# Expert tiles of a mixture-of-experts layer loaded and stored in pairs, their slots interleaved in DRAM

## The reference, cut to what matters

```python
xn = layernorm(x)                                   # 2048 tokens x 256
router = sigmoid(xn @ gate_w)                       # 16 experts
selected = top_k(router + expert_bias, 2)           # two experts for each token
top_scores = router[selected] / sum                 # their weights
shared = silu(xn @ sg_w) * (xn @ su_w) @ sd_w       # one expert that every token takes
for e in range(16):
    g, u = split(xn @ experts_gate_up[e])           # 256 -> 2 x 128
    routed += comb[:, e] * (silu(g) * u @ experts_down[e])
return x + attention(xn) + shared + routed
```

## Time and profile before

| | |
|---|---|
| time, median of 3 runs | 526.53 us (524.24 to 529.89) |
| profiled execution, time and span | 525.04 us, 523.2 us |
| PE busy | 461.9 us (88%) |
| DVE busy | 324.3 us (62%) |
| ACT busy | 249.4 us (48%) |
| POOL busy | 198.4 us (38%) |
| `x_in<-sorted_tokens` | 48 loads of 128 KB, median 2.7 us from issue to landing |
| `sorted_outputs<-y_out` | 48 stores of 128 KB, median 1.7 us |

### The profile page before, as it was taken

One profiled execution on the slowest core, in us unless ns is written; L12 is line 12 of the kernel. 1 busy time (PEld: TensorE's weight loads), 2 busy tenths in 40 slices (PEclk: granted clock), 3 DMA queues, 4 the chain that ended last, 5 costly groups with the idle time before them and its releaser, 6 DMA issues.

```text
span 523.2 us, 9031 instructions
## 1 busy us (share of the span) xinstructions
PE 461.9 (88%) x3049; PEld 271.6 (52%) x3050; DVE 324.3 (62%) x610; ACT 249.4 (48%) x567; POOL 198.4 (38%) x239
## 2 busy tenths in 40 slices
PE   4595999737859999995999999999999999999998
PEld 4454788525635666763445354444444444332676
DVE  3869985413425656676867877778586867744232
ACT  2620652112213333332767676676676757678300
POOL 3470777699940000006888888800000000000000
PEclk9799799977779999997999999999999999999999
DMA  9898999799999434424113333221120000010022
GB/s 282 188 403 256 318 323 291 246 170 144 188 174 203 127 110 121 130 79 140 42 49 104 108 86 106 71 76 61 48 82 18 3 3 3 1 13 6 3 89 73
DMA packets 65705, 64.60 MB, mean 123 GB/s; under 512 B 21935, under 2 KB 59539, under 8 KB 65635
## 3 DMA queue, kind: packets, MB, share of 16 engines
q1 hardware_dynamic: 51506, 47.85, 30.9%
q0 software_dynamic: 13056, 15.83, 15.0%
q10 hardware_dynamic: 1104, 0.41, 0.3%
HBM read 37.27 MB, written 27.13 MB: 123 GB/s over the span
## 4 chain that ended last, share of the span: by engine, by line
PE 66%; DVE 13%; DMA 12%; issue 2%; ACT 2%; POOL 2%; SPq 1%; POOLq 0%; DVEq 0%
PE ps L1248 12%; PE ps L1222 10%; PE ps L1234 10%; PE ps L1147 7%; PE ps L1268 5%; DMA x_in<-sorted_tokens 5%; DVE mx L970 5%; PE ps L1043 4%; PE ps L1163 4%; DMA ks<-aux_rows 2%; PE ps L1237 2%; PE ps L1223 2%; PE ps L1137 2%; ACT pt L718 2%; DMA x_sb<-x 1%
## 5 line engine op out<-in xcount | busy, mean ns | idle before, releaser
L718 ACT ACTIVATE pt<-ps 128x512 f32<-128x512 f32 (+3 forms) x384 | 167.1, 494 | 79.7 <-PE ps L1237 55.2
L970 DVE TENSOR_REDUCE mx<-ps 128x1 f32<-128x384 f32 (+6 forms) x189 | 153.3, 863 | 52.4 <-PE ps L1223 51.1
L1248 PE MATMUL ps<-pt,vg 128*32 128x512 f32 (+3 forms) x768 | 71.9, 492 | 0.0
L575 POOL DMA_INDIRECT yg<-sorted_outputs,slot_i x32 | 32.0, 1000 | 94.2 <-DMA sorted_outputs<-y_out 85.4
L1147 PE MATMUL ps<-w_gu,hx 128*128 x192 | 58.3, 432 | 3.8 <-issue 2.2
L1234 PE MATMUL ps<-qs,ks 111*128 111x512 bf16 (+3 forms) x192 | 55.7, 331 | 3.7 <-DMA qs<-nr 3.0
L1234 PE MATMUL ps<-qk 111*128 111x512 bf16 (+3 forms) x192 | 54.9, 329 | 1.8 <-ACT pt L718 0.3
L935 DVE COPY y_out<-ps 128x256 f32<-128x256 f32 x48 | 20.4, 425 | 56.4 <-PE ps L1163 52.7
L1237 PE MATMUL ps<-cbf 128*128 128x128 bf16 x256 | 52.4, 221 | 0.0
L691 ACT ACTIVATE hx<-ps 128x384 f32<-128x384 f32 (+1 forms) x48 | 22.9, 477 | 61.3 <-PE ps L1137 58.6
L1222 PE MATMUL ps<-qk 108*128 108x512 bf16 (+3 forms) x192 | 50.2, 328 | 1.8 <-DVE mx L970 1.3
(11 more groups left out here) (175 smaller groups left out, 737.9 us busy)
## 6 DMA issues: line engine op xcount, KB each, us to landing
sorted_tokens<-y_out SPq DMA_DIRECT2D x12, 512.0 KB, 5.0
qk_parts<-parts SPq DMA_DIRECT2D x16, 384.0 KB, 3.5
x_in<-sorted_tokens SPq DMA_DIRECT2D x48, 128.0 KB, 2.7
sorted_outputs<-y_out SPq DMA_DIRECT2D x48, 128.0 KB, 1.7
w_gu<-e_gu SPq DMA_DIRECT2D x1, 2816.0 KB, 12.9
x_sb<-x SPq DMA_DIRECT2D x4, 512.0 KB, 8.4
w_dn<-e_dn SPq DMA_DIRECT2D x1, 2048.0 KB, 8.7
y<-x_sb SPq DMA_DIRECT2D x16, 128.0 KB, 1.7
```

The source lines that it names most:

```text
L575: g_.indirect_dma_start(out=yg[:, n % 4, :], out_offset=None, in_=ysd, in_offset=bass.IndirectOffsetOnAxis(ap=slot_i[:, k, t:t + 1], axis= ...
L718: sc.activation(pt[:, s % 4, j, lo:CH], bank(n % 3)[:, lo:CH], ACT.Exp).then_inc(s_exp, 1)
L970: last = v.reduce_max(dst, src, axis=AX.X)
L1248: ins = te.matmul(ps[32 * j:32 * j + 32, OUT_BANK * CH + lo:(OUT_BANK + 1) * CH], vg[:, par, kb, j, :], pt[:, s % 4, j, lo:CH], start=kb = ...
```

## The change: two tiles to a transfer

Two consecutive tiles (2m and 2m + 1) share a block of 256 rows in DRAM. Before, slot s is row s. Now row 2p + b of the block belongs to partition p of tile 2m + b, so that one partition's two rows lie side by side, 2 KB. VectorE computes the new row number from the slot with integer operations (5 more instructions than the cast before), SP loads and stores two tiles with one DMA each, and there are two semaphores for the loads and two for the stores where there were four of each. The buffers stay four; a pair of them is loaded, and stored, at once. The gather reads the same rows through `slot_i`.

```diff
+            slot_n = tmp("slot_n", [P, 3, K_TOP, TT], I32)
...
-        s_xin = [sem(f"tile_loaded{i}") for i in range(4)]
+        s_xin = [sem(f"tile_pair_loaded{i}") for i in range(2)]
...
-        s_ys = [sem(f"tile_out_stored{i}") for i in range(4)]
+        s_ys = [sem(f"tile_pair_stored{i}") for i in range(2)]
...
-            def load_tile(k, u):
-                sp.dma_start(x_in[:, u, :], xsd[bass.ds(k * P, P), :]).then_inc(s_xin[u], DMA)
-
-            def store_tile(k, u):
-                sp.wait_ge(s_yo, k + 1)
-                sp.dma_start(ysd[bass.ds(k * P, P), :], y_out[:, u, :]).then_inc(s_ys[u], DMA)
-
-            for k in range(4):
-                load_tile(k, k)
+            def load_tiles(k, half):
+                sp.dma_start(x_in[:, 2 * half:2 * half + 2, :],
+                             xsd[bass.ds(k * P, 2 * P), :].rearrange("(p k) d -> p k d", k=2)).then_inc(s_xin[half], DMA)
+
+            def store_tiles(k, half):
+                sp.wait_ge(s_yo, k + 2)
+                sp.dma_start(ysd[bass.ds(k * P, 2 * P), :].rearrange("(p k) d -> p k d", k=2),
+                             y_out[:, 2 * half:2 * half + 2, :]).then_inc(s_ys[half], DMA)
+
+            for half in range(2):
+                load_tiles(2 * half, half)
...
-            def next_tile(k, u):
-                sp.wait_ge(s_hxt, k - 3)
-                load_tile(k, u)
-
-            for k in range(4, 7):
-                next_tile(k, k % 4)
+            def next_tiles(k, half):
+                sp.wait_ge(s_hxt, k - 2)
+                load_tiles(k, half)
+
+            next_tiles(4, 0)
             with sp.Fori(0, NT // 4 - 2) as i:
-                for u in range(4):
-                    next_tile(i * 4 + u + 7, (u + 3) % 4)
-                    store_tile(i * 4 + u, u)
-            next_tile(NT - 1, 3)
-            for k in range(NT - 8, NT):
-                store_tile(k, k % 4)
+                for half in range(2):
+                    next_tiles(i * 4 + 2 * half + 6, 1 - half)
+                    store_tiles(i * 4 + 2 * half, half)
+            next_tiles(NT - 2, 1)
+            for k in range(NT - 8, NT, 2):
+                store_tiles(k, k // 2 % 2)
...
-                v.tensor_copy(slot_i[:, :, :], slot_f[:, :, :]).then_inc(s_slot, 1)
+                then(v.tensor_copy(slot_n[:, 0, :, :], slot_f[:, :, :]))
+                then(v.tensor_scalar(slot_n[:, 1, :, :], slot_n[:, 0, :, :], P - 1, 1,
+                                     ALU.bitwise_and, ALU.logical_shift_left))
+                then(v.tensor_scalar(slot_n[:, 2, :, :], slot_n[:, 0, :, :], 7, 1,
+                                     ALU.logical_shift_right, ALU.bitwise_and))
+                then(v.tensor_tensor(slot_n[:, 1, :, :], slot_n[:, 1, :, :], slot_n[:, 2, :, :], ALU.bitwise_or))
+                then(v.tensor_scalar(slot_n[:, 0, :, :], slot_n[:, 0, :, :], 8, 8,
+                                     ALU.logical_shift_right, ALU.logical_shift_left))
+                v.tensor_tensor(slot_i[:, :, :], slot_n[:, 0, :, :], slot_n[:, 1, :, :], ALU.bitwise_or
+                                ).then_inc(s_slot, 1)
...
-                    dve.wait_ge(s_ys[u], stored)
+                    dve.wait_ge(s_ys[u // 2], stored)
...
-                pe.wait_ge(s_xin[u], need)
+                pe.wait_ge(s_xin[u // 2], need)
```

More of the change, by code:

```diff
@@ L563, in _ @@
                         load(pool, side, g, half)
-            for u in range(4):
-                pool.wait_ge(s_ys[u], NT // 4 * DMA)
+            for stored in s_ys:
+                pool.wait_ge(stored, NT // 4 * DMA)
             pool.wait_ge(s_sha, TT // 2)
```

## The result

Over four runs of each on the same chip the changed kernel takes 538.17 us (534.75 to 540.67), the kernel before 525.38 us (523.81 to 529.89): ratio 1.0225, 95% interval 1.0132 to 1.0318. The forecast was 525.5 us with a range of 515 to 533; the time lies outside it, on the side of rival B and beyond its price. The profiled execution took 540.67 us, the longest of the four, with a span of 538.8 against 523.2; so the two profiles lie 15.6 us apart where the medians lie 12.8 apart.

The account below looks back on a forecast made before the run. Mostly PE bound it, with tile loads waiting beside POOL's queue early in the tile stage. 525.04 + 1.05 (slots) - 1.2 (paired loads) = 524.9, or 526.4 on the median's scale; stated 525.5 us, range 515 to 533.

Parts of the forecast that it names:

- rival B: SP's ring of two pairs: lost look-ahead outweighs the gain, landing takes 12.7 us; slower, 533 us, chance 0.20.
- What bounds the kernel: Chain mostly PE, 66%; tile loads matter only at the tile stage's start, beside POOL's queue, 5% of the span.
- four tiles take L' + 2.3 (a step) + 0.4: Crowded tile stage: paired landing time plus one step plus SP and transpose, 12.4 us per four tiles; gain 1.2 us.
- L': A paired load's time to landing in the crowded part, taken as 9.7 us, between 7.2 and 12.7.
- Tile 8 itself: First paired load in the crowd: issued at about 122.0, landing 10.4 us later, tile 8 at 132.4.
- The step: Time from a pair's first tile to its second on PE, taken as 2.3 us.
- Rival A: DMA queues taking turns by packet: pairs drain faster, landing falls to 7.2 us; faster, 517 us, chance 0.33.
- Rival C: SP's queue cuts each 2 KB into 1 KB packets, landing stays 14.4 us; slower, 534 us, chance 0.05.
- The slots, +1.05 us: Five added VectorE instructions before the scatter, 0.21 us each, delay the path in full by 1.05 us.
- First scores until 118: PE's first attention scores would wait for POOL's loads until 118 us, neither much longer nor shorter.
- The quiet part, 0: From tile 20 on PE sets the pace; paired loads and stores land within three steps, so no effect, 0.
- Stores: Under rival B: DVE may wait for a paired store issued one step later; no size of its own.

Follow-up runs that it names:

- e9: The kernel before with six input buffers in place of four, single tiles loaded six steps ahead: 522.66 us, ratio 0.9956 to the kernel before.
- e4: The kernel before, layout and 1 KB packets kept, with two single-tile loads issued together as a pair, stores likewise: 532.47 us, ratio 1.0132.
- e2: The changed kernel with loads in pairs but stores of single tiles: 537.03 us, ratio 1.0182 to the kernel before.
- e10: The kernel before with six input buffers and POOL's loads spread over the stage: 511.89 us, ratio 0.9761 to the kernel before.
- e3: The changed kernel with stores in pairs but loads of single tiles: 526.22 us, ratio 0.9996 to the kernel before.
- e8: The changed kernel with single-tile stores and each load pair issued as two transfers of 1 KB packets: 531.51 us, ratio 1.0162 to the kernel before.
- e12: e8 with PE waiting until both tiles of a pair have landed: 535.41 us, ratio 1.0205 to the kernel before.
- e1: The changed kernel's slots and row layout only, with loads and stores of single tiles: 527.23 us, ratio 1.0081 to the kernel before.
- e7: The changed kernel with six input buffers, three pairs, in place of four: 521.71 us, ratio 0.9957 to the kernel before.
- e5: The kernel before with POOL's loads for later head groups spread over tile steps: 513.90 us, ratio 0.9837 to the kernel before.
- e6: The changed kernel with POOL's loads for later head groups spread over tile steps: 531.49 us, ratio 1.0167 to the kernel before.

## Why the prediction was wrong

- **What bounds the kernel: right.** Tile loads beside POOL's queue, in the first third of the stage, and nowhere else.
- **The step that failed** is "four tiles take L' + 2.3 (a step) + 0.4" with L' taken as 9.7 us. The form held; every term of it was too small. From the rows of tiles 8 to 12: the step from tile 8 to tile 9 was 138.52 to 142.98, 4.46; SP's issue came 0.95 after the transpose; L' was 14.51. The sum is 20.0 against 12.4. The next circle, tiles 12 to 16, parts the terms: there L' was 9.62, the figure of the forecast, and it still took 14.7 us, since the step took 4.13 and SP's issue 0.85.
- **Tile 8 itself** came at 138.52 us where I had 132.4. Tile 5 was transposed 4.2 us later than in the kernel before (125.02), for the later start and the later first scores below; the load went out 1.7 after it, behind the store of tiles 0 and 1 in SP's order, and not 1.2; and it took 11.71, not 10.4.
- **L'.** I took the landing time to be set by how many of SP's transfers are in flight, and so chose the lightly loaded 9.7 where the earlier trace rows had 14.4 for this very stretch. The runs refute that: 12.3 us with six buffers in flight (e9), 13.5 for pairs of single loads (e4), 11.71 and 14.51 for the 2 KB pairs, the latter issued with no other tile load under way. Of the loads issued between 118 and 150 us the medians are 12.1 us before, 11.7 in the changed kernel, and 11.3 to 13.8 in the runs with POOL's loads all at once, however the transfers are cut. The first paired load took 11.71, already at the point (11.8) that I had named as decisive.
- **The step.** 2.3 us is PE's pace in the quiet part. In this stretch PE has just stood idle, runs at 1.2 GHz (granted clock 0.50 from 138 to 143 us), and does some of the first attention scores between two transposes. The kernel before shows the same: tile 8 at 131.07, tile 9 at 135.37; and tiles 4 and 5, 3.3 us apart, stood in the earlier trace rows when I took 2.3. With single buffers it cost the loads little, because the load of tile 12 went out ahead of it (131.94). The pair put it on the path.
- **Rival B was the way it went**, with its place, the ring of two pairs on SP, and priced too low: 533, since it took 12.7 for L' and the same 2.3 for the step. The chance of 0.20 was too small: it asked for no more than 12.7, less than the 14.4 that the stretch showed, and the forecast needed L' to fall by a third.
- **Rival A, quicker draining: refuted.** SP's packets did become half as many, for the same bytes in the same 14 us, with less engine time. L' did not fall. The Trainium skill, page "DMA: Bandwidth & Descriptors", section "Queues, rings and completion order", has each engine take turns between queues by packet, a packet there being some 9 to 17 descriptors. Whether these are the packets that the profile counts, no run here shows; my step from the turns to a shorter landing is what the traces contradict. Its section "Rules for kernel authors" says to coalesce many small transfers into one large one; here the transfers were of 128 KB to begin with, and coalescing the loads (e2, with the new slots and rows) cost 1.8%.
- **Rival C: refuted.** 558 packets carried what 1118 had.
- **The slots, +1.05 us: right.** Six instructions stand where one was (53.26 to 54.54 us), 0.22 apart, 1.1 us in all. The rest of the 2.7 us by which the first load is later is no effect of it: `place` itself began at 46.8 us in the kernel before and at 48.7 in the changed one, but also at 48.7 in e10, which has no new slots.

```profile
53.26 0.18 DVE L879 CAST slot_n<-slot_f 128x32 int32<-128x32 f32 x1
53.47 0.18 DVE L880 TENSOR_SCALAR slot_n<-slot_n 128x32 int32<-128x32 int32 x1
...
54.35 0.19 DVE L887 TENSOR_TENSOR slot_i<-slot_n 128x32 int32<-128x32 int32 x1
```

- **First scores until 118: missed by little.** Their loads came at 107.82 + 13.84 = 121.66 us, of which 1.9 us are a longer landing, not the later start. That landing is 10.2 to 13.8 us over the runs, in no order that goes with the change, so I take it for scatter; no run settles it.
- **The quiet part, 0: about right.** Tiles 24 to 47 took 50.2 us against 49.0, and PE waited for no tile load there. The 1.2 us are not explained.
- **Stores: the wait came, and loads hid it.** I named DVE's wait for a paired store under rival B; it came (15.5 us). In the changed kernel it is not on the chain. e3 shows that it is there as soon as the loads are single: by itself it then costs what the wait for single loads had cost, so the time stays.

What stays open: between e4 (1.0132) and the change (1.0225) lie the slots, 1.1 us, and probably the wait for both tiles' bytes, some 2 us by e8 and e12. The intervals do not part them. Whether rows 2 KB apart cost e1 something beside its slots isn't settled either, nor what a wider output ring would give.

## What to carry to other kernels

Before transfers are joined in a ring of fixed size, count the look-ahead, not the transfers: a pair is asked for when its second buffer is free and is needed at its first, which takes one step from a ring of four, and the step to count is the slow one that follows a stall. The same holds for the ring of stores, which took the chain over wherever the loads no longer held it (e3, e7, e9). Take the landing time from the row of the very stretch, not from a lonelier one, unless something shows that it falls. And when a ring binds, first ask what makes the landing long: here two more buffers gave 0.4%, the other queue's loads spread in time 1.6%, and both together 2.4%.

## What the hardware showed that I had not expected

- A tile load issued beside POOL's full queue, between 118 and 150 us, takes 8 to 16 us to land, with medians of 11.3 to 13.8 in the ten kernels that issue POOL's loads all at once, whether 128 KB or 256 KB, in packets of 1 or 2 KB, from a ring of four buffers or of six (e7, e9). In the quiet it takes 2.1 or 2.7 us. One group of four POOL loads just ahead of it is enough for 6 to 8 us (e5, e6).
- Packets of 2 KB take less engine time for their bytes: in the crowd 0.298 x 16 x 14 / 558 = 120 ns each, where those of 1 KB took 79 (means over all of q1's packets in 131 to 145 us); a quarter less for the same data. It made no transfer land earlier.
